# Squares of both Newton lanes on four quadrants, and token chunks regrouped, in a fused vision block

## The reference

```
tokens = patchify(concat(x, four one-pixel shifts of x), 16)   # 2048 tokens x 3840
h  = layernorm(tokens; gamma, beta) @ W + b                    # 2048 x 192
a  = layernorm(h); q, k, v = heads of (a @ w_qkv.T)            # 12 heads of 16, 64 tokens per image
K1 = K2 = K3 = softmax(q k.T / 4)                              # one landmark per token
V  = K2.T / max column sum
6 times: V = 0.25 V (13 I - KV (15 I - KV (7 I - KV))),  KV = K2 V
h += (K1 V (K3 v)) @ w_proj.T + b_proj
h += mixture of 16 experts, top 8 of a softmax router, gelu, on layernorm(h)
```

## Time and profile before

| | |
|---|---|
| median of 3 runs | 698.87 us (697.99 to 701.11) |
| profiled execution | 700.34 us, its span 698.5 us |
| mean granted TensorE clock | 0.990 |
| PE busy | 648.6 us, 93% of the span |
| DVE / ACT / POOL busy | 494.8 (71%) / 384.6 (55%) / 105.7 (15%) us |
| transfers | 30.64 MB, mean 44 GB/s |

### The profile page before, as it was taken

One profiled execution on the slowest core, in us unless ns is written; L12 is line 12 of the kernel. 1 busy time (PEld: TensorE's weight loads), 2 busy tenths in 40 slices (PEclk: granted clock), 3 DMA queues, 4 the chain that ended last, 5 costly groups with the idle time before them and its releaser, 6 DMA issues.

```text
span 698.5 us, 29941 instructions
## 1 busy us (share of the span) xinstructions
PE 648.6 (93%) x13218; PEld 570.8 (82%) x13218; DVE 494.8 (71%) x1351; ACT 384.6 (55%) x1045; POOL 105.7 (15%) x328
## 2 busy tenths in 40 slices
PE   4678999999999989999999898899999999999997
PEld 2567888888888878888888787688999999999996
DVE  5557878878888888888888877576557457556743
ACT  0236666676766666676676666755333344444332
POOL 1302123113223212212212301110000000000000
PEclk9889999999999999999999999999999999999999
DMA  8793111121121121121100000000000000000000
GB/s 309 264 252 106 34 65 34 34 64 34 34 64 35 34 63 34 34 64 35 34 4 4 5 4 4 5 2 0 1 23 1 1 0 23 2 1 23 1 1 23
DMA packets 13409, 30.64 MB, mean 44 GB/s; under 512 B 1248, under 2 KB 7520, under 8 KB 13024
## 3 DMA queue, kind: packets, MB, share of 16 engines
q1 hardware_dynamic: 13280, 28.73, 12.9%
HBM read 27.16 MB, written 1.57 MB: 41 GB/s over the span
## 4 chain that ended last, share of the span: by engine, by line
PE 84%; DVE 6%; ACT 3%; issue 2%; DVEq 0%; ACTq 0%
PE ps L398 28%; PE ps L562 18%; PE ps L552 16%; PE ps L289 5%; PE ps L305 2%; PE ps L365 2%; PE ps L416 2%; PE ps L347 2%; PE ps L306 2%; PE ps L339 1%; DVE uu L844 1%; DVE rf L851 1%; PE ps L429 1%; DVE se L800 1%; DVE sst L798 1%
## 5 line engine op out<-in xcount | busy, mean ns | idle before, releaser
L903 DVE SCALAR_TENSOR_TENSOR acc<-ps,comb,acc 128x192 f32<-128x192 f32 x256 | 89.1, 410 | 83.9 <-PE ps L562 83.8
L562 PE MATMUL ps<-w_sb,work 128*128 128x192 f32 x768 | 140.4, 326 | 0.7 <-ACT work L731 0.7
L562 PEld LDWEIGHTS ps<-w_sb,work 128*128 128x128 f32 x768 | 129.5, 189 | 9.5 <-issue 1.1
L731 ACT ACTIVATE work<-ps 128x512 f32<-128x512 f32 x96 | 57.3, 597 | 137.8 <-PE ps L552 137.8
L398 PEld LDWEIGHTS ps<-rr 64*64 64x64 f32 x3840 | 98.2, 135 | 22.9 <-issue 14.7
L398 PE MATMUL ps<-rr 64*64 64x64 f32 x3840 | 110.9, 223 | 6.4 <-issue 5.3
L844 DVE SCALAR_TENSOR_TENSOR uu<-rr,qq 128x384 f32<-128x384 f32 x160 | 86.5, 563 | 32.9 <-ACT qq L637 25.8
L398 PE MATMUL ps<-uu,qq 64*64 64x64 f32 x4608 | 96.0, 224 | 11.0 <-DVE uu L844 10.2
L644 ACT ACTIVATE rr<-ps 128x384 f32<-128x384 f32 x160 | 73.4, 489 | 56.3 <-PE ps L398 55.9
L398 PEld LDWEIGHTS ps<-uu,qq 64*64 64x64 f32 x4608 | 80.8, 134 | 26.4 <-DVE uu L844 16.1
L641 ACT ACTIVATE qq<-ps 128x384 f32<-128x384 f32 x96 | 47.1, 491 | 8.8 <-PE ps L398 3.0
(11 more groups left out here) (142 smaller groups left out, 1066.7 us busy)
## 6 DMA issues: line engine op xcount, KB each, us to landing
xtb<-xt_dram SPq DMA_DIRECT2D x16, 512.0 KB, 3.5
work<-x_dram SPq DMA_DIRECT2D x16, 512.0 KB, 3.7
wsh<-ws_dram SPq DMA_DIRECT2D x10, 288.0 KB, 5.5
w_sb<-w_dram SPq DMA_DIRECT2D x1, 2304.0 KB, 23.4
w_a<-w_dram SPq DMA_DIRECT2D x1, 1536.0 KB, 11.5
w_b<-w_dram SPq DMA_DIRECT2D x2, 768.0 KB, 15.9
out_dram<-acc SPq DMA_DIRECT2D x4, 384.0 KB, 2.6
mult<-copies_dram SPq DMA_DIRECT2D x1, 512.0 KB, 8.3
```

The lines of the kernel that those rows point to most:

```text
L562: last = pe.matmul(ps[:, 2 + 2 * (e % 2) + j // 2, (j % 2) * DIM:(j % 2 + 1) * DIM], hid[:, n % 4, j * P:(j + 1) * P], w2_sb[:, c, :], sta ...
L731: act.activation(hid[:, n % 4, :], ps[:, UPB[n % 3], :], ACT.Gelu_apprx_tanh).then_inc(gelu_done, 1)
L903: last = dve.scalar_tensor_tensor(out=a, in0=ps[:, 2 + 2 * (e % 2) + j // 2, (j % 2) * DIM:(j % 2 + 1) * DIM], scalar=comb[:, g * GT + j, ...
```

## The change

Lane 1's squares are crossed in the same steps as lane 0's, with three copies on ACT in place of one; the count of `q_ready` goes from 4 to 6 per step. Of the eight token chunks of a tile the first two stay in step 1's first place, three (instead of two) stand in step 2's first place, and three in step 3's first place, ahead of `transpose_sums` and `gram`; step 2's second place is empty on PE.

```diff
-CROSSED = (1, 2, 3, 5)
+CROSSED = ((1, 2, 3, 5), (1, 2, 3, 5))
...
-                            crossed = i == 1 and (phase == 1 or lane == 0 and k in CROSSED)
+                            crossed = i == 1 and (phase == 1 or k in CROSSED[lane])
...
                 if k == 2 and on(t + 3):
-                    tok(t + 3, 2, 4)
+                    tok(t + 3, 2, 5)
+                if k == 3 and on(t + 3):
+                    tok(t + 3, 5, CH)
                 if k == 3 and on(t + 1):
                     transpose_sums(t + 1)
                     gram(t + 1)
...
-                if k == 2 and on(t + 3):
-                    tok(t + 3, 4, CH)
...
-                    if lane == 0 and k in CROSSED:
-                        act.activation(q[:, 0], ps[:, 0, 0:LC], ACT.Copy).then_inc(q_ready, 1)
+                    if k in CROSSED[lane]:
+                        act.activation(q[:, 0], ps[:, 2 * lane, 0:LC], ACT.Copy).then_inc(q_ready, 1)
                         for a in (0, 64):
-                            act.activation(q[a:a + 64, 1], ps[64 - a:128 - a, 1, 0:LC], ACT.Copy).then_inc(q_ready, 1)
-                    elif lane == 0:
-                        act.activation(q, ps[:, 0:2, 0:LC], ACT.Copy).then_inc(q_ready, 3)
+                            act.activation(q[a:a + 64, 1], ps[64 - a:128 - a, 2 * lane + 1, 0:LC],
+                                           ACT.Copy).then_inc(q_ready, 1)
                     else:
-                        act.activation(q, ps[:, 2:4, 0:LC], ACT.Copy).then_inc(q_ready, 1)
+                        act.activation(q, ps[:, 2 * lane:2 * lane + 2, 0:LC], ACT.Copy).then_inc(q_ready, 3)
...
-                dve.wait_ge(q_ready, 4 * (STEPS * t + k) + 3 + lane)
+                dve.wait_ge(q_ready, 6 * (STEPS * t + k) + 3 * lane + 3)
```

## The result

The changed kernel takes 709.21 us (median of 4 runs, 706.36 to 713.83) against 699.58 us for the kernel before (4 runs): ratio 1.0123, interval 1.0091 to 1.0156. It is slower by 9.6 us. The forecast was 701.5 us, with a range of 694 to 708, so 2.6 us more than the 698.87 us known then: the side it leaned to was right, the size was little over a quarter of the real one.

A forecast was written before the change was run, and what follows sets the result against it. It took the ACT-DVE chain between square and product, nearly level with PE, to bind steps 2 and 3. Terms -0 - 1.0 - 0.5 + 4.0 + 0.5 = +3.0 us on 700.34 gave 703.3, 701.9 on the median; forecast 701.5, range 694 to 708.

The forecast's parts named there:

- The last three iterations lose: Iterations 13 to 15, without chunks: lane 1's longer copies cost 0.8, 1.2 and 2.0 us, together 4.0.
- four bare 0.5's: Iteration 15: in four steps each 0.5 us of lane 1's longer copies goes straight on the path, 2.0 us.
- the rivals: PE's gain shows, about 690 us (chance 0.20); instruction pauses, 708 (0.13); ACT queues longer than counted, 706 to 707 (0.17).
- A usual iteration: Iterations 1 to 12: 0.21 - 0.12 - 0.24 + 0.14 = -0.01 us each, nothing.
- Step 1: Usual iteration: lane 1's copies hold exponents and copy_out, so project starts later; 0.21 us lost.
- step 5: Usual iteration, no chunk, qk covers the copies: last DVE operations start earlier, 0.24 us won, 0.14 given back.
- Steps 2 and 3: Usual iteration: one chain through copies and U sets the time, 8.77 us against 8.89, 0.12 won, not 0.66.
- Step 0: Next iteration's start: lane 0 released 0.24 us earlier, lane 1 only 0.10, so 0.14 of step 5's gain given back.
- Pauses: Step 1 pauses in five iterations hide ACT's delay, 1.0 us won; instruction supply in steps 2 to 3, 0.5 added.
- The rival of more pauses: Steps 2 to 3: instruction supply can't follow, a pause in most iterations, 6.5 us on top, 708; chance 0.13.
- Iteration 0: Slice with a lower granted clock, where halving the squares' cost gives more: 0.5 us won, between 0 and 1.5.
- the undecided terms: Whole sum: they lean down more easily than up, so 701.5 us was said instead of 701.9.

The follow-up runs named there:

- the first kernel: Changed kernel with the token chunks back in their old places, four in step 2's second place, lane 1 still crossed: 719.24 us, ratio 1.0278.
- the sixth: Changed kernel with idle matmuls on PE in the first places of steps 2 to 5 of iteration 15: 707.58 us, ratio 1.0112.
- the third: Changed kernel with PE computing lane 1's squares on two quadrants, ACT still making three copies (straight, not crossed): 707.76 us, ratio 1.0100.
- DVE's copies: Changed kernel with DVE copying image 0's part of both lanes' squares in steps 2, 3 and 5: 700.47 us, ratio 1.0032.
- the squares alone: Changed kernel with one ACT copy for lane 1's crossed squares, image 1's halves not put back: 687.62 us, ratio 0.9815.

## Why the prediction was wrong

The picture was right: PE's gain is waited out, the copies set the time, step 1 gains nothing, and the last iterations lose. The size failed, in one step above all.

1. *"The last three iterations lose ... Together 4.0 us."* They lost 8.7: 2.2, 1.6 and 4.9 where 0.8, 1.2 and 2.0 had been counted. This is the step that failed. The chain part was mis-sized, about 5.6 for 4.0 (iteration 15: about 2.8 for the 2.0 counted as four bare 0.5's; lane 1's squares now also follow lane 0's by 0.79 us in steps 1 and 3, where it was 0.64 and 0.52). Two things were left out of it. One is the fall of the clock, about 2.1 us, though the sum itself made PE stand still longer there (4.1 us of iteration 15 before, 7.1 now). The other is 1.0 us by which step 0 of iteration 13 was longer than the 4.11 us of the iterations ahead of it, mostly a pause of 0.74 in the scores without a releaser. I named the clock nowhere among the rivals. Part of the 8.7 belongs to this one profile: with the same work in these iterations the first kernel took 77.48 us there and the sixth, filler and all, 77.40, against 78.68.
2. *"A usual iteration comes to ... nothing."* It grew by 0.35 us, 25.65 for 25.30. Step 1, forecast +0.21, was 4.91 for 4.69, and step 5, forecast 3.92, was 3.94. Steps 2 and 3 were 8.96, not 8.77: every link of the chain was there, most of them a few hundredths longer, and U of lane 1 took 0.66 us instead of 0.58, which the rows of before already showed (two in 1.15, rows 4). Step 0 gave back 0.22 instead of 0.14, and step 4, which I had left alone, grew by 0.06. Twelve times 0.35 is 4.2 us.
3. *Pauses: 1.0 won in step 1, 0.5 lost.* The twelve iterations grew by 1.2, so 3.0 of the 4.2 came back: beyond their shortest they held 6.2 us before (309.83 less 12 x 25.30) and 3.2 now (311.02 less 12 x 25.65). The idle time put down to "issue" (PE waits for nothing that the profile shows) ahead of line 398 fell from 33.9 to 14.2 us, that put down to DVE's U rose from 26.3 to 64.3. One wait may have hidden the other, but that isn't shown: the kernel before, with its instructions only shifted, also held no more than 3.1 us beyond its shortest (306.83 less 12 x 25.31). So that the twelve iterations lost only 1.2 us here is in part luck. The rival of more pauses did not happen.
4. *Iteration 0: 0.5 won.* It was 2.0 (27.52 to 25.49). The half-clock stretch that lay in it before had ended ahead of it in the changed kernel's profile; most of this is where the low clock fell, and so perhaps are the 2.2 lost in the set-up.
5. *"the undecided terms lean down more easily than up (a chain of handoffs is often a little shorter than the sum of its parts)"*. The reverse was seen, in every term of point 2. The 0.4 us taken off for it weighed little; the upper end of 708 allowed for one mishap at a time, and here several came together.

In the profiles the sum is 2.2 - 2.0 + 1.2 + 8.7 = 10.1 us, the difference of the spans; forecast were 0 - 0.5 - 0.5 + 4.0 = 3.0. The first two terms have no tie to the change that a run here shows. The runs decide between the other two: undone in the last three iterations alone, the change costs 0.2 to 1.4 us (ratios 1.0003 and 1.0020).

## What to carry to other kernels

Where a faster operation needs a dearer hand-over, price the hand-over as latency and find each place where nothing covers it; the loops' last passes, whose fillers have run out, are such a place, and three of sixteen held most of the loss here. A wait that is added where PE is already thin can cost twice, as in iteration 15, once in time and once in clock. To see whether a gain is real, run its two halves apart: the gain without its price (0.9815) and the price without its gain (1.0100) told more than the whole (1.0123).

## What had not been expected of the hardware

In the changed kernel the clock fell after 390 us at full, in iteration 15. It did so in that iteration in all six profiles with lane 1's longer copies there: the mean granted over the iteration was 0.81 of full in the changed kernel, 0.93 with the filler, 0.87 in the first kernel, 0.93 in the third, 0.86 with DVE's copies and 0.71 with step 1 uncrossed. In the four other profiles that end with lane 1 uncrossed, and in that of the kernel before, it stayed full. With the squares alone it fell there too (0.93), and once more in iteration 4 (0.94), after a pause of 0.92 us without a releaser. So a fall isn't bound to the copies, and where in the iteration it comes differs from profile to profile.

ACT's three copies of a crossed square follow each other at 0.35 us without overlap, as forecast from the earlier trace rows, while the two copies of `copy_out`, on the same engine, start 0.16 us apart and last 0.26 each (214.18 and 214.34 in the changed kernel); DVE's copy of 128x192 took 0.345 us. With 128 PE instructions more in the set-up, pauses of 0.7 to 1.3 us stood in other iterations, though, as said, some of them also come and go between executions.
